# Layer 3's feed-forward network as one pipeline per sequence, row stores on ScalarE's queue, and the loop over pairs written out

## The reference

```python
gates = softmax(xt @ gate_w)                  # 8 experts
top_v, top_i = top_k(gates, 2);  top_v = top_v / sum(top_v)
h  = gelu(einsum('nd,edf->enf', xt, fc_w))    # 128 -> 512
eo = einsum('enf,efd->end', h, proj_w)        # 512 -> 128
out = sum(eo[top_i] * top_v)
```

## Time and profile before

| | |
|---|---|
| time, median of 3 runs | 1465.61 us (1464.19 to 1466.54) |
| the profiled execution | 1464.16 us, of which the span 1462.3 us |
| first pair, second pair (by the span) | about 30 to 748 us, 748 to 1462 us |
| layer 3's tiles in the span | about 372 to 453 us and 1090 to 1171 us |
| PE busy in 300 to 400 us, 400 to 500 us | 98.05 us, 74.40 us |
| granted clock in the same | 1.00, 0.88 |

### The profile page before, as it was taken

The page is one execution under the profiler, slowest core; times in us unless marked ns, Lnnn a source line. Parts: engine busy times, 40 slices in busy tenths (PEclk is TensorE's granted clock), DMA queues, the critical chain, the costliest instruction groups (busy, mean ns, idle before and its releaser), DMA issues.

```text
span 1462.3 us, 26184 instructions
## 1 busy us (share of the span) xinstructions
PE 1310.0 (90%) x8544; PEld 1075.9 (74%) x8544; DVE 757.9 (52%) x2099; ACT 706.2 (48%) x1486; POOL 203.6 (14%) x195
## 2 busy tenths in 40 slices
PE   6898999999966988989978989999998869798998
PEld 5586577778965855879947856777887857577898
DVE  3785444565314746753256835445642256475532
ACT  2764455555432454454447535555553324544553
POOL 1054100002223101000011620000202320020000
PEclk8999999999998999999989999999998989999999
DMA  6000000004573000000000000000227430000000
GB/s 267 1 1 1 1 1 1 1 1 157 167 243 148 1 1 1 5 1 15 1 17 1 1 1 1 1 1 1 104 76 231 165 139 1 1 1 1 1 8 8
DMA packets 30405, 65.10 MB, mean 45 GB/s; under 512 B 3358, under 2 KB 19008, under 8 KB 29504
## 3 DMA queue, kind: packets, MB, share of 16 engines
q1 hardware_dynamic: 27504, 55.46, 11.0%
q0 software_dynamic: 2048, 4.20, 0.9%
q10 hardware_dynamic: 720, 3.72, 0.7%
HBM read 54.33 MB, written 9.04 MB: 43 GB/s over the span
## 4 chain that ended last, share of the span: by engine, by line
PE 52%; issue 29%; POOL 8%; DVE 5%; DMA 3%; ACT 2%; SPq 0%; DVEq 0%; POOLq 0%; ACTq 0%
PE psum L742 45%; PE psum L776 7%; POOL arenaA L1394 2%; POOL probs L1412 2%; DMA outs_dram<-arenaC 1%; POOL rs L1350 1%; DMA moe<-in_w_folds_dram 1%; POOL rows_dram L1386 1%; POOL arenaD L1365 1%; POOL probs L1406 1%; DVE xn L1473 1%; DVE arenaA L1798 1%; DMA arenaA<-rows_dram 0%; DMA rows_dram<-xn,row_at 0%; DVE stat L1449 0%
## 5 line engine op out<-in xcount | busy, mean ns | idle before, releaser
L1125 ACT ACTIVATE arenaB<-psum 128x512 f32<-128x512 f32 x448 | 167.8, 426 | 110.4 <-PE psum L776 109.1
L742 PE MATMUL psum<-moe,arenaA 128*128 128x128 f32 x1504 | 187.6, 279 | 14.5 <-DVE arenaC L1729 11.6
L1125 ACT ACTIVATE arenaA<-psum,vec 128x512 f32<-128x512 f32 (+1 forms) x208 | 125.3, 614 | 154.4 <-PE psum L742 154.0
L742 PE MATMUL psum<-arenaD,arenaB 128*128 128x128 f32 (+2 forms) x1440 | 188.3, 279 | 8.3 <-ACT arenaB L1125 7.6
L742 PEld LDWEIGHTS psum<-moe,arenaA 128*128 128x128 f32 x1504 | 180.5, 195 | 19.3 <-DVE arenaC L1729 12.0
L742 PEld LDWEIGHTS psum<-arenaD,arenaB 128*128 128x128 f32 (+1 forms) x1440 | 173.8, 194 | 16.2 <-issue 7.8
L1125 ACT ACTIVATE probs<-probs,nmax 128x589 f32<-128x589 f32 x128 | 100.8, 787 | 168.5 <-DVEq L1596 168.0
L1593 DVE CUSTOM_DVE_ANT_0 probs<-psum,shift 128x589 f32<-128x589 f32 x128 | 98.7, 771 | 145.9 <-PE psum L742 143.1
L776 PE MATMUL psum<-w_first,probs 128*128 128x128 f32 (+2 forms) x1120 | 161.8, 275 | 12.1 <-POOL probs L1412 6.9
L776 PEld LDWEIGHTS psum<-w_first,probs 128*128 128x128 f32 (+2 forms) x1120 | 131.3, 144 | 34.3 <-issue 24.2
L742 PE MATMUL psum<-seen,qh 128*128 128x512 f32 (+1 forms) x512 | 154.5, 424 | 1.6 <-ACT qh L1125 1.6
(11 more groups left out here) (230 smaller groups left out, 2004.1 us busy)
## 6 DMA issues: line engine op xcount, KB each, us to landing
moe<-in_w_moe_dram SPq DMA_DIRECT2D x60, 512.0 KB, 4.9
moe<-in_w_moe_dram SPq DMA_DIRECT2D x2, 4096.0 KB, 14.6
outs_dram<-arenaC SPq DMA_DIRECT2D x12, 320.0 KB, 5.6
moe<-in_w_folds_dram SPq DMA_DIRECT2D x3, 1024.0 KB, 10.5
arenaA<-rows_dram SPq DMA_DIRECT2D x4, 640.0 KB, 5.2
rows_dram<-arenaB SPq DMA_DIRECT2D x2, 960.0 KB, 17.1
w_l<-in_w_l_dram ACTq DMA_DIRECT2D x1, 1500.0 KB, 13.0
arenaA<-rows_dram SPq DMA_DIRECT2D x4, 320.0 KB, 3.4
```

The costliest lines, as they stand in the source:

```text
L742: return nc.tensor.matmul(out, lhsT, rhs, start=start, stop=stop, skip_group_check=shared)
L1125: return nc.scalar.activation(out, in_, func, **kw)
```

## The change

The list of steps of layer 3 is rearranged, and some steps change engines:

- The second sequence's `norm_stats` and `norm_apply` come before tile step 2, its gates and `places` keep their distance in the list to one step, and DVE gives the rows to POOL (`rows_known`) before it works out the experts of the tiles.
- The two sequences are two pipelines of 17 steps each (m = 0 to 16 and 17 to 33). The second starts when the first has run empty.
- ACT issues the stores of the rows (in groups of 6, 6 and 3 tiles), and the load of sequence 1's tiles (in parts of 3 and 12 tiles); SP keeps the loads of the weights and of sequence 0's tiles.
- `rows_back(0)` stands at m = 17, `combine(0)` at m = 28; `rows_back(1)` at unit 0 of layer 4, `combine(1)` at unit 6.
- `project_heads` is split into `project_context` (keys and values, which need only the context) and `project_queries`. Both sequences' `project_context` of layer 4 stand at m = 16 and 17.
- Layer 6's two masking matmuls of a unit come after both score matmuls.
- The loop over pairs is written out on all engines, so that every wait compares with a constant.

```diff
-NB3, GROUP3 = 8, 5
+NB3 = 8
+SENDS3 = [(0, 6), (6, 12), (12, 15)]
+SEND_AFTER = [10, 15, 16]
...
     def rows_step(m):
-        if m < len(ROWS3):
-            do("row_turn", *ROWS3[m], m, wide())
-        if 1 <= m <= len(ROWS3):
-            do("row_hidden", *ROWS3[m - 1], m - 1, wide())
+        s, m = m // (TILES3 + 2), m % (TILES3 + 2)
+        if m < TILES3:
+            do("row_turn", s, m, TILES3 * s + m, wide())
+        if 1 <= m <= TILES3:
+            do("row_hidden", s, m - 1, TILES3 * s + m - 1, wide())
         if m >= 2:
-            do("row_out", *ROWS3[m - 2], m - 2, gen())
+            do("row_out", s, m - 2, TILES3 * s + m - 2, gen())
+        if m in SEND_AFTER:
+            do("send_rows", s, SEND_AFTER.index(m))
...
         if k == n + 4:
             do("heads_out", 1, G0)
+            norm_stats(3, 1)
+            norm_apply(3, 1)
...
-    between = {2: (lambda: norm_stats(3, 1),), 3: (lambda: norm_apply(3, 1),), 4: (lambda: norm_turn(3, 1),),
-               5: (lambda: do("logits", 3, 1, gen()), lambda: gates(3, 1, 0)), 6: (lambda: gates(3, 1, 1),),
-               7: (lambda: gates(3, 1, 2), lambda: do("places", 1, gen()), lambda: do("rows_out", 1)),
-               18: (lambda: do("rows_back", 0),), 20: (lambda: do("sum_columns", 0), lambda: do("sum_columns", 1)),
-               24: (lambda: do("combine", 0), lambda: norm_stats(4, 0)), 25: (lambda: norm_apply(4, 0),),
-               27: (lambda: norm_turn(4, 0),),
-               30: (lambda: do("project_heads", 4, 0, gen(), turn(), turn(), big()),)}
-    for m in range(2, len(ROWS3) + 2):
-        rows_step(m)
+    between = {5: (lambda: norm_turn(3, 1),), 6: (lambda: do("logits", 3, 1, gen()), lambda: gates(3, 1, 0)),
+               7: (lambda: gates(3, 1, 1), lambda: gates(3, 1, 2)),
+               9: (lambda: do("places", 1, gen()), lambda: do("rows_out", 1)),
+               13: (lambda: do("sum_columns", 0), lambda: do("sum_columns", 1)),
+               16: (lambda: do("project_context", 4, 0, gen(), big()),),
+               17: (lambda: do("project_context", 4, 1, gen(), big()), lambda: do("load_rows", 1),
+                    lambda: do("rows_back", 0)),
+               28: (lambda: do("combine", 0), lambda: norm_stats(4, 0)), 29: (lambda: norm_apply(4, 0),),
+               31: (lambda: norm_turn(4, 0),), 33: (lambda: do("project_queries", 4, 0, turn(), turn()),)}
+    for m in range(2, NS * (TILES3 + 2)):
         for step in between.get(m, ()):
             step()
+        rows_step(m)
...
-    small_attention(4, {1: (lambda: do("rows_back", 1),), 4: (lambda: do("combine", 1), lambda: norm_stats(4, 1)),
-                        5: (lambda: norm_apply(4, 1),), 6: (lambda: norm_turn(4, 1),),
-                        7: (lambda: do("project_heads", 4, 1, gen(), gen(), turn(), big()),),
+    small_attention(4, {0: (lambda: do("rows_back", 1),), 6: (lambda: do("combine", 1), lambda: norm_stats(4, 1)),
+                        7: (lambda: norm_apply(4, 1),), 8: (lambda: norm_turn(4, 1), lambda: do("project_queries", 4, 1, turn(), turn())),
...
-                    if n in (NB3 - 1, 17):
-                        load_rows(int(n == 17))
-                    if n >= NB3 and (n - NB3) % GROUP3 == GROUP3 - 1:
-                        send_rows((n - NB3) // GROUP3)
-                send_rows(4)
-                send_rows(5)
+                    if n == NB3 - 1:
+                        load_rows(sp, 0)
...
+            def send_rows(s, g):
+                a, b = SENDS3[g]
+                act.wait_ge(*reader_did("ro", TILES3 * s + b - 1))
+                at = 128 * sent_at(s, a)
+                act.dma_start(dram[f"outs{s}"][128 * a:128 * b, :].rearrange("(j p) d -> p j d", p=128),
+                              sent_rows[:, at:at + 128 * (b - a)].rearrange("p (j d) -> p j d", d=128))\
+                    .then_inc(rows_sent[s][g].sem, 16)
+
+            def take_rows(s):
+                load_rows(act, s)
...
-            with act.Fori(0, PAIRS) as pair:
+            for pair in range(PAIRS):
```

More of the change, by code:

```diff
@@ L81, in at @@
     def at(self, *event):
-        return self.value(self.order.get(event, 1) + self.credit)
+        return self.value(self.order.get((self.it[0],) + event, 1) + self.credit)
     def value(self, n):
-        it = self.it[0]
-        return (self.sem, it * self.known.get("total", 0) + n)
+        return self.sem, n
 S0, S1, T0, T1, G0, G1 = range(6)
@@ L585, in program @@
         weights_in = [signal(f"weights_in_{b}") for b in range(NB3)]
-        rows_sent = [signal(f"rows_sent_{h}") for h in range(2)]
+        rows_sent = [[signal(f"rows_sent_{s}_{g}") for g in range(3)] for s in range(NS)]
+        rows_known = signal("rows_known")
         gathered = [signal(f"gathered_{s}") for s in range(NS)]
@@ L645, in parts_free, with load_rows @@
                 eng.wait_ge(*tensor_did("hid", *PARTED[n - 2], FT - 1))
+        def load_rows(eng, s):
+            eng.wait_ge(scattered[s].sem, it[0] * 128 + 128)
+            for h, (a, b) in enumerate(((0, 3), (3, TILES3))):
+                eng.dma_start(xg[s][:, 128 * a:128 * b].rearrange("p (j d) -> p j d", d=128),
+                              dram[f"rows{s}"][128 * a:128 * b, :].rearrange("(j p) d -> p j d", p=128)).then_inc(rows_in[s][h].sem, 16)
         NSMALL = 3
@@ L718, in _ @@
                 sp.dma_start(dram[f"rows{s}"].rearrange("(p j) d -> p (j d)", p=128), arenaB[:, 0:128 * TILES3]).then_inc(cleared.sem, 16)
[L719 to L721 removed]
+            for pair in range(PAIRS):
+                pair_moves(pair, pair == PAIRS - 1)
             it[0] = 0
@@ L837, in scores @@
                         last = mm(slot(i, 4 * KEYS, at=512 * r), rot[s][:, 0, t * 128:(t + 1) * 128],
-                                  kbd[s][:, h:h + 4, :].rearrange("p j k -> p (j k)"), stop=l == 4)
-                        if l == 6:
-                            last = mm(slot(i, 4 * KEYS, at=512 * r), ident_r[:, :], barred[:, t, :], start=False)
+                                  kbd[s][:, h:h + 4, :].rearrange("p j k -> p (j k)"), stop=l == 4, shared=l == 6)
+                    if l == 6:
+                        for r in range(2):
+                            last = mm(slot(i, 4 * KEYS, at=512 * r), ident_r[:, :], barred[:, t, :], start=False, shared=True)
                 last.then_inc(*filled[i].mark("sc", l, s, hf, t))
@@ L1113, in _ @@
             fold()
-            with pe.Fori(0, PAIRS) as pair:
+            for pair in range(PAIRS):
                 it[0] = pair
@@ L1151, in head_norm @@
                 act.wait_ge(*filled[i].at("q0", s, k))
-                if prev_sq[0] is not None:
+                if prev_sq[0] is not None and (s, k) != TILES0[0]:
                     act.wait_ge(*hsum_ready.at(*prev_sq[0]))
@@ L1389, in rows_back @@
             def rows_back(s):
-                for g in range(3 * s, 3 * s + 3):
-                    pool.wait_ge(*group_sent(g))
+                for g in range(3):
+                    pool.wait_ge(*group_sent(s, g))
                 pool.sem_inc(held_pool.sem, 1)
@@ L1421, in _ @@
             pool.wait_ge(consts_ready.sem, 6)
-            with pool.Fori(0, PAIRS) as pair:
+            for pair in range(PAIRS):
                 it[0] = pair
@@ L1713, in places @@
                 for n in range(2):
-                    v.tensor_tensor(picked[n], taken[n], at, ALU.mult)
+                    ins = v.tensor_tensor(picked[n], taken[n], at, ALU.mult)
+                link(ins)
+                for n in range(2):
+                    ins = v.tensor_reduce(rows[:, 4 * n:4 * n + 4], picked[n], AX, ALU.add)
+                link(ins)
+                v.tensor_copy(row_at[:, s, :], rows).then_inc(*rows_known.mark(s))
                 link(v.tensor_tensor(by_tile, last.unsqueeze(1).broadcast_to([128, 16, E]),
                                      vec[:, places_at:places_at + 16].unsqueeze(2).broadcast_to([128, 16, E]), ALU.is_le))
-                for n in range(2):
-                    v.tensor_reduce(rows[:, 4 * n:4 * n + 4], picked[n], AX, ALU.add)
                 link(v.tensor_reduce(owner, by_tile, AX, ALU.add))
-                v.tensor_copy(row_at[:, s, :], rows)
                 v.tensor_scalar(expert_at[:, s, :], owner, float(E - 1), None, ALU.min).then_inc(*placed.mark(s))
             def row_out(s, j, n, i):
-                g = n // GROUP3
-                if n % GROUP3 == 0 and g >= 2:
-                    dve.wait_ge(*group_sent(g - 2))
+                if s == 1 and j in (6, 12):
+                    dve.wait_ge(*group_sent(0, j // 6 - 1))
                 dve.wait_ge(*filled[i].at("ro", n))
-                a = 128 * (n % (2 * GROUP3))
+                a = 128 * sent_at(s, j)
                 v.tensor_copy(sent_rows[:, a:a + 128], slot(i, 128)).then_inc(*free[i].mark("ro", n))
@@ L1758, in project_heads, with project_queries @@
                     v.tensor_scalar(kk, slot(i, KEYS), V("kb3"), None, ALU.add).then_inc(*free[i].mark("kv", l, s))
```

(12 more changed lines are left out.)

74 lines of the change are left out of this document (31 added, 43 removed).

## The result

The changed kernel takes 1449.24 us (median of four runs, 1444.35 to 1453.16), the kernel before 1466.07 us in the same comparison. The ratio is 0.9886, with a 95% interval of 0.9861 to 0.9910: 17 us faster. Forecast were 1431 us and a range up to 1447, so half of the gain came and the time lies outside. The profiled run after is the shortest of the four, 1444.35 us with a span of 1442.2.

A forecast was written before the change was run, and what follows sets the result against it. PE (90% busy) bounds the kernel, so gains lie in its waits and half clock. Rebuilt stage 29.4 us, loop's turn 4, register instructions 1, layer 6 -0.8: 33.6 us less, 1431 us forecast, range 1413 to 1447.

The forecast's parts named there:

- Combination of sequence 1: Layer 4: the store-to-gather chain remains, DVE combines two units later, PE's wait falls from 11.4 to 5.5 us a pair.
- Rows of sequence 1: Layer 3's tiles: scatter ends no later, load on ACT; wait and refill 4.0 us a pair, plus 0.5 us of clock.
- Clock after combination 1: Layer 4: half clock on PE after its wait for sequence 1's combination still costs 2.5 us a pair.
- Gates, combination of sequence 0, rotated queries, unit 8: PE's waits in layer 3's tiles and layer 4's start: 0.2, 1.3, 0.9 and 2.4 us a pair would remain.
- The stage as a whole: Layer 3's tiles and layer 4's start: 17.3 us lost a pair instead of 32, so 14.7 us gained.
- The loop's turn: Between the two pairs: DVE starts 3.6 us earlier and half a microsecond of clock is added, 4 us gained once.
- Rival C: The gap at the loop's turn stays in the written-out code: 4 us less gain, 1435 us; chance 0.11.
- Register instructions: 748 of 32 ns on one PE line disappear: 1 us gained for both pairs, 0 to 8 kept possible.
- rival B: Hand-offs gain from constants: some 300 on PE's path save 50 ns each, 15 us more, 1416 us; chance 0.13.
- Layer 6: Queries behind the values delay its first scores, 0.4 us lost a pair; moving the masking matmuls gives 0.
- rival D: ACT's stores and loads crowd out weights and lengthen tile steps; slower, 1473 us at 2.6 us a step; chance 0.05.
- Rival E: Waits move: sequence 1's row load, gathers for `combine(0)` and clock lose 4 + 5 + 3 us a pair; 1455 us; chance 0.13.

The follow-up runs named there:

- e2: Changed kernel, but SyncE's large load (4096 KB of expert weights) waits until sequence 1's last row store has landed; 1435.57 us, ratio to before 0.9781.
- e4: Changed kernel with row stores and load of sequence 1's rows back on SyncE's queue, last two stores ahead of the large load; 1427.68 us, ratio to before 0.9732.
- e6: Kernel of e1 with the large load put ahead of sequence 1's last row store on SyncE's queue; 1480.28 us, ratio to before 1.0099.
- e5: Kernel of e3, but the large load waits until sequence 1's gathers have landed; 1417.27 us, ratio to before 0.9660.
- e3: Kernel of e2, with SyncE also holding back weights of sequence 1's tile 3 until the first part of its rows has landed; 1421.81 us, ratio to before 0.9698.
- e1: Kernel before, its schedule kept, with only the loop over pairs written out on all engines; 1455.76 us, ratio to before 0.9926.

## Why the prediction was wrong

The step that failed is in "Combination of sequence 1": "That chain remains (store of three tiles instead of five, no weights beside it)". Weights were ahead of it. (They were beside it before, too: the large load was issued 0.44 us behind the last store and ran beside the gathers, but behind the store it did the store no harm.) The prediction followed each row transfer to its new queue, but not SP's list without them: with the stores gone, SP's next item was the large load, and it was issued 0.76 us before the store. In "Rows of sequence 1" the same fault stands as "The scatter ends no later now": it took 5.80 instead of 2.23 us in the first pair and 4.71 instead of 4.15 in the second. e2 to e4 took the cause away in different ways and the time followed; e6 brought it into the old kernel.

Term by term, for a pair:

- **Combination of sequence 1**, 5.5 us forecast, 15.1 measured. In e5, with nothing beside the chain, 4.0. This term alone lost 9.6 us.
- **Rows of sequence 1 and the clock after them**, 4.5 us forecast. Measured: the wait of 5.1 us, the refill's 0.2, and lost clock. After PE's return three eights of matmuls and a transpose take 417.28 - 411.87 = 5.4 us, and 2.8 at full clock (0.9 for each eight, 0.1 for a transpose). Together 7.9, 3.4 us too little forecast: the wait and the refill, 5.3 us, lie within their bounds of 1.5 and 8, the 2.6 us of clock above theirs of 1.6. In the second pair it is 4.9, 0.2 and 1.3 us, together 6.4. The store ahead of the load on ACT, which the sum priced, was covered by the later scatter and shows only in e3.

```profile
410.98 0.69 PE L779 MATMUL psum<-w_first,arenaA 128*128 128x128 f32 x2 [5.06 <-DMA arenaA<-rows_dram]
411.87 2.05 PE L745 MATMUL psum<-arenaA,moe 128*128 128x128 f32 x8 [0.20 <-issue]
...
417.28 0.27 PE L779 MATMUL psum<-w_first,arenaA 128*128 128x128 f32 x1
```

- **Clock after combination 1**: 2.5 us forecast. From PE's return at 479.28 us on, the granted clock is 0.50 (1.2 GHz). Against the same shapes at full clock this costs, as an estimate, some 4 us in the first pair and 2 us in the second, where the clock is back before the four matmuls on `seen` (first pair, second pair):

```profile
484.47 3.78 PE L745 MATMUL psum<-seen,w_l 128*128 128x512 f32 x4 [0.69 <-ACT seen L1131]
...
1189.35 1.99 PE L745 MATMUL psum<-seen,w_l 128*128 128x512 f32 x4 [0.69 <-ACT seen L1131]
```

- **Gates, combination of sequence 0, rotated queries, unit 8**: forecast 0.2, 1.3, 0.9 and 2.4 us. Measured: no wait, 1.1, 0.6, and 0.7 + 1.5 = 2.2. These were right.
- **The stage as a whole.** 14.7 us a pair were forecast. e3, with the weights held back at both places, gains 122.2 - 107.7 = 14.5 and 123.2 - 108.3 = 14.9. So the schedule holds what the sum gave it, and the changed kernel lost it to the weights. That e3 comes so near is in part luck: its wait for the combination is 7.2 us instead of 5.5, because the gathers still meet the large load, and its wait for the rows is 2.1 us, where the sum had 4.0 with the refill. e5, whose store and gathers meet no large load, as the sum assumed, gains 17.3 and 17.6. (The sum also took 25 + 6.6 as 32, 0.4 us a pair too much.)
- **The loop's turn**: 4 us forecast, 3.7 measured (e1). Rival C falls: without the loop the gap is shorter by about the 3611 ns that the taken branch showed. The Trainium skill, Runtime: NRT & Kernel Launch, "Instruction fetch mechanics", says that a taken branch to a place outside the stretch of code that an engine holds has to wait until it is fetched. No run here shows whether that was the cause.
- **Register instructions**: 1 us taken, 0 to 8 kept. e1's 10.9 us less the turn's 3.7 leave 7 (3 to 11). In e1's profiled run it is 5 us (1453.7 against 1462.3 of span, less the turn). The value taken was too low by 4 to 6 us. The sum had counted the 748 instructions of one line on PE; the written-out e1 has 2945 instructions fewer than before on all engines (23239 against 26184). The gain is a third to a half of what rival B gave its constants; that it comes from them, and not from something else in the written-out code, is not shown.
- **Layer 6**: a loss of 0.4 us a pair was forecast; the stretch got 2.0 shorter, and 0.6 of this is e1's as well. The other 1.4 are shorter waits of PE for DVE and ACT (5.2 us in e1, 3.8 after), not the masking matmuls: a masked unit takes 3.05 us in e1 and 3.04 after. The wrong sign, on a small term.

The two errors have opposite signs. In the profiled runs the stage gave 22.6 us less than the 29.4 forecast, and the rest some 9 more than its 4.2, so 20.1 us of span are gained instead of 33.6. That is 13.5 of the 18 us between 1431 and 1449.24. The other 5 us lie in the median, which stands 4.9 us over the profiled run after and 1.5 to 1.9 over that of before; the four runs differ in the mean granted clock (0.976 in the shortest, 0.969 in the longest), and why is open.

The sharing of the DMA engines was weighed in the prediction for the wrong thing: for the load's own duration, and as rival D for the tile steps. Those stayed at 1.90 us (421.07 to 422.96 from transpose to transpose). What it bears on is a small transfer with a waiting engine behind it: with the large load issued ahead, the store took 13.36 us from another engine's queue (after) and 12.45 us from the same (e6). The Trainium skill, DMA: Bandwidth & Descriptors, "Issuing engines are not separate DMA queues", says that DMAs of several engines interleave on the same DMA engines. The runs agree: a queue of its own did not spare the store. Rival E came nearest in time (1455), with the row load's delay at the right place, but its gathers for `combine(0)` were in time.

After, the first pair's stage is 2.8 us longer than the second's (120.7 against 117.9). The clock accounts for it: it came back 1.3 us of work later after the rows' wait (5.4 against 4.1 us for the same matmuls) and 1.8 us later after the combination's (3.78 against 1.99 us on `seen`). Open are why the clock came back at different times after waits of the same length, and the share of the register instructions in what the written-out code gains.

## What to carry to other kernels

A queue that waits also holds back everything behind it in its list, and this can be what keeps bulk loads away from short transfers on the critical path. Before transfers move to another engine, write down what the old engine will issue in their place, and when. Issued half a microsecond behind the short transfer a bulk load did no harm here; issued 0.8 us or more ahead it cost some 10 us. Where a bulk load has time, make it wait for the landing of the short transfers (here the load of the rows behind the scatter, then the store and its gathers): such waits took the changed kernel from a ratio of 0.9886 to 0.9660.

## What the runs showed of the hardware

- The last store took 2.1 us from the copy's end to its landing when the 4096 KB load waited for it (192 KB, e2), and 2.1 and 2.9 us when that load was issued 0.4 us behind it (192 KB, e4; 320 KB, before). It took 13.4 and 12.5 us when the load had been issued 0.8 and 1.9 us ahead of it, on another engine's queue (after) and on the same (e6). In these two it landed 0.3 and 0.8 us after the load, which took 13.8 and 13.5 us.
- The last gather by indirect DMA landed 2.5 to 2.7 us after its issue when no large load was under way (after, e5, e6), and 5.8 to 6.0 us when one had been issued 9.7 us before it (e2, e3); there it landed 0.9 us after the load. The scatter's last one took 2.2 us with the DMA engines nearly idle (before and e4, first pair) and 4.7 to 5.8 us beside loads of 512 KB (after, both pairs).
- After 5.1 us of standing PE ran at a granted clock of 0.50 (1.2 GHz) for 5.4 us; in e3, after 2.1 us, it came back at once (eight matmuls in 1.13 us).
